# Edge scores of a graph attention layer: row one-hots made three sets ahead, and pieces of rows handed back a step later

## The reference, cut to what matters

```python
Q = relu(x @ query_kernel + query_bias)[row]      # one row of 128 per edge
K = relu(x @ key_kernel + key_bias)[col]
att = sum(Q.reshape(-1, 8, 16) * K.reshape(-1, 8, 16), axis=-1)   # 8 scores per edge
alpha = segment_softmax(att, row, 6250)
```

## Time and profile before

| what | value |
|---|---|
| median of three runs | 10467.82 us |
| the profiled execution's own time | 10462.73 us |
| its span | 10461.2 us |
| the stage, first to last VectorE one-hots or reduce | 2342.9 to 3404.8 us |
| VectorE busy in 2342 to 3405 us | 972.79 us of 1063 |
| TensorE busy in the same stretch | 925.54 us |
| ScalarE busy in the same stretch | 664.03 us |
| GpSimd busy in the same stretch | 55.06 us |
| granted TensorE clock in the stretch | 1.00 |

### The profile page before, as it was taken

One profiled execution on the slowest core, in us unless ns is written; L12 is line 12 of the kernel. 1 busy time (PEld: TensorE's weight loads), 2 busy tenths in 40 slices (PEclk: granted clock), 3 DMA queues, 4 the chain that ended last, 5 costly groups with the idle time before them and its releaser, 6 DMA issues. The chain is left out here.

```text
span 10461.2 us, 308127 instructions
## 1 busy us (share of the span) xinstructions
PE 8085.6 (77%) x93666; PEld 6641.9 (63%) x93814; DVE 8031.5 (77%) x16702; ACT 4527.8 (43%) x9123; POOL 1394.2 (13%) x1711
## 2 busy tenths in 40 slices
PE   2335666758888456999986998898999779579996
PEld 0232225547777446999984666346999746378886
DVE  4987777779999666666667998777888777788887
ACT  0220002236666114666654443786777556323333
POOL 0110001210000002666550000000000012100000
PEclk7555555559999557999998999999999989889998
DMA  2000004424444112333324887785555400000000
GB/s 55 0 7 8 5 5 141 147 77 163 161 162 155 38 37 81 123 123 121 124 95 162 271 273 245 259 292 159 144 144 144 115 5 6 3 4 3 3 3 14
DMA packets 613317, 1065.91 MB, mean 102 GB/s; under 512 B 120883, under 2 KB 266554, under 8 KB 606967
## 3 DMA queue, kind: packets, MB, share of 16 engines
q1 hardware_dynamic: 489222, 890.58, 26.8%
q10 hardware_dynamic: 113040, 161.93, 4.2%
q0 software_dynamic: 10976, 12.53, 0.4%
HBM read 868.94 MB, written 195.84 MB: 102 GB/s over the span
## 5 line engine op out<-in xcount | busy, mean ns | idle before, releaser
L2548 POOL TENSOR_TENSOR acc<-acc,m_sum 128x544 f32<-128x544 f32 (+1 forms) x637 | 811.0, 1273 | 1225.5 <-ACT m_sum L2515 1185.2
L2412 DVE TENSOR_TENSOR m_msg<-m_vps,m_msg 128x512 f32<-128x512 f32 (+1 forms) x637 | 427.7, 671 | 409.4 <-PE m_vps L2453 371.2
L2477 PE MATMUL m_sps<-m_msg,m_oh 128*128 128x136 f32 x4900 | 697.5, 286 | 0.0
L2884 PE MATMUL u_sps<-u_r,u_oh 128*128 128x129 f32 x4900 | 657.2, 275 | 28.7 <-ACT u_r L2840 28.7
L1545 ACT COPY sp_adj_x<-sp_aps_x 128x512 f32<-128x512 f32 (+1 forms) x637 | 363.0, 570 | 724.2 <-PE sp_aps_x L1516 724.2
L1532 PE MATMUL sp_out_x<-x,sp_adj_x 128*128 128x128 f32 x4802 | 672.8, 284 | 0.0
L1516 PE MATMUL sp_aps_x<-sp_ohw_x,sp_oh_x 128*128 128x128 bf16 x7350 | 537.3, 221 | 166.1 <-DVE sp_ohw_x L1483 166.0
L2117 PE MATMUL s_qps<-q_parts,s_oht 128*128 128x128 bf16 x7203 | 511.5, 220 | 198.6 <-DVE s_oht L1599 146.9
L2868 PE MATMUL u_zps<-fcs,u_a 128*128 128x128 f32 x4916 | 655.1, 276 | 7.2 <-ACT u_a L2833 7.2
L2884 PEld LDWEIGHTS u_sps<-u_r,u_oh 128*128 128x128 f32 x4900 | 599.0, 192 | 37.6 <-issue 37.6
L2477 PEld LDWEIGHTS m_sps<-m_msg,m_oh 128*128 128x128 f32 x4900 | 609.9, 190 | 0.0
(11 more groups left out here) (590 smaller groups left out, 19682.3 us busy)
## 6 DMA issues: line engine op xcount, KB each, us to landing
u_e<-e_tiles SPq DMA_DIRECT2D x591, 256.0 KB, 2.8
e_tiles<-t_es ACTq DMA_DIRECT2D x588, 256.0 KB, 4.2
g_e<-e_tiles SPq DMA_DIRECT2D x588, 256.0 KB, 4.5
s_rows<-bucket_rows SPq DMA_DIRECT2D x148, 768.0 KB, 4.1
m_rows<-bucket_rows SPq DMA_DIRECT2D x148, 768.0 KB, 4.1
bs_krow<-bucket_keys SPq DMA_DIRECT2D x49, 1600.0 KB, 7.0
t_rows<-bucket_rows SPq DMA_DIRECT2D x148, 384.0 KB, 5.2
s_rows<-bucket_rows SPq DMA_DIRECT2D x49, 896.0 KB, 5.1
```

Source lines behind the costliest of these rows:

```text
L2477: last = nc.tensor.matmul(sps[x][:, at:at + M], oh[x][:, j * P:(j + 1) * P], msg[x][:, j * M:(j + 1) * M], start=True, stop=True)
L2548: nc.gpsimd.tensor_tensor(at, at, sums[x][:, 0:n * M], ALU.add).then_inc(added, 1)
L2884: last = nc.tensor.matmul(sps[:, :], oh[x][:, j * P:(j + 1) * P], zr[x][:, j * D1:(j + 1) * D1], start=(q == 0 and j == 0), stop=(q == las ...
```

## The change

The one-hots are made for step q + 3 and no longer for q + 2 (`AHEAD = 3`), in the same ring of three slots and a spare one; three sets are made ahead of the first window. Handing a piece back (the waits for `oht_made` and `act_made`, and the increment of `rows_free`) becomes a function of its own, `give_back`, which runs behind the reduce of the same step and no longer between the one-hots and the reduce. For the first three sets it runs ahead of the loop. On ScalarE the wait for the ring slot (`k_made`) moves from ahead of Square to ahead of Relu, and both work for step q + 3.

```diff
-    last_q = NQ - 1
+    last_q, AHEAD = NQ - 1, 3
@@ vector
                     else:
                         row_hots(nc, k, B, oht[r], buf[n], q).then_inc(oht_made[r], 1)
+
+                def give_back(w, q):
+                    n, r = piece_of(B, q), O.slot(q)
                     if q + 1 == B.pieces[n][1]:
                         dve.wait_ge(oht_made[r], O.before(w, q) + 1)
                         here = [p for p in shared if p < B.pieces[n][1]]
                         if here:
                             dve.wait_ge(act_made, w * len(shared) + (len(here) + 1))
                         dve.sem_inc(rows_free[n], 1)
...
-                first_hots(0)
-                first_hots(1)
+                for q in range(AHEAD):
+                    first_hots(q)
+                for q in range(AHEAD):
+                    give_back(0, q)
                 with dve.Fori(0, nw) as w:
...
                         nc.vector.tensor_tensor(prod[x]..., qs[x]..., kps[x]..., ALU.mult).then_inc(prod_made[x], 1)
-                        if q + 2 < NQ:
-                            hots(w, q + 2)
-                        else:
-                            hots(w + 1, q + 2 - NQ)
+                        wp, p = (w, q + AHEAD) if q + AHEAD < NQ else (w + 1, q + AHEAD - NQ)
+                        hots(wp, p)
                         dve.wait_ge(prod_made[x], X.before(w, q) + 2)
                         n = B.held(q)
                         nc.vector.tensor_reduce(...).then_inc(summed[x], 1)
+                        give_back(wp, p)
@@ scalar
-                        p, n = q + 2, w * len(shared)
+                        p, n = q + AHEAD, w * len(shared)
                         if p in shared:
-                            back, user = O.user_before(p)
                             act.wait_ge(rows_in[piece_of(B, p)], w * 16 + 16)
-                            act.wait_ge(k_made[X.slot(user)], X.before(w, user) + (1 + k0 + back * X.uses[X.slot(user)]))
                             act.wait_ge(act_made, n + (shared.index(p) + 1))
                             nc.scalar.activation(far[:, :], row_of(1, p), ACT.Square, bias=minus[:, 0:1]).then_inc(far_made, 1)
                         act.wait_ge(q_made[x], X.before(w, q) + 1)
                         act.wait_ge(prod_made[x], X.before(w, q) + 1)
                         nc.scalar.copy(qs[x]..., qps[x]...).then_inc(q_copied[x], 1)
                         if p in shared:
+                            back, user = O.user_before(p)
                             act.wait_ge(far_made, n + shared.index(p) + 1)
+                            act.wait_ge(k_made[X.slot(user)], X.before(w, user) + (1 + k0 + back * X.uses[X.slot(user)]))
                             nc.scalar.activation(oht[O.slot(p)][:, GE:], far[:, :], ACT.Relu, bias=1.0, scale=-1.0).then_inc(act_made, 1)
```

## The result

The changed kernel takes 10409.68 us (median of 5 runs, 10406.45 to 10416.37) against 10465.63 us of the kernel before in the same comparison (5 runs): a ratio of 0.9946, 95% interval 0.9932 to 0.9961. It is faster by 56 us. The forecast was 87 us faster, 10381 us; the measured time lies just past the end of the range, 10408. The direction and the mechanism named for the gain hold, the size does not: 31 us are missing.

What follows compares the result with a forecast made beforehand. VectorE was taken to bound the stage, but for one wait per window at its seam. Four hand-backs of 0.445 us save 1.78 us per window, 87 us over 49: 10467.8 - 87 = 10381 us, range 10370 to 10408.

Steps and rivals of the forecast that it cites:

- The value of the hand-back: VectorE: handing back behind the reduce saves 0.445 us at four places per window, 87 us over 49 windows.
- the slow one-hots beside GpSimd's copy: VectorE one-hots taking 0.57 for 0.48 us beside GpSimd's copies: forecast to stay; if they missed, 4 us more won.
- One-hots three ahead ... I cost this at nothing: TensorE's waits for one-hots go, but VectorE didn't wait on them, so the longer lead was priced at nothing.
- The seam stays: From multiply 12 to multiply 0 of the next window: k group 0 still waits for multiply 12, 1.51 us as before.
- I take nothing: Waits of a hand-back, now ahead of the next multiply, cost nothing; a satisfied wait at most 0.02 us.
- the forecast period of 19.83 us: Time from multiply 0 to multiply 0 of the next window: 21.61 us less 1.78 us for four hand-backs.
- my third rival: At the seam, TensorE's longer pause lets the clock fall and the kernel gets slower, up to 10980 us; chance 0.02.
- the 1.9 us of pause: At the seam, TensorE finishes q group 0 earlier and waits about 1.9 us for multiply 12, where it paused 1.34.
- the slack of 3.7 us per window: TensorE's spare time per window: its groups need 16.1 us against VectorE's new 19.83.
- The first rival: Part is taken back: hand-back instructions not quite hidden, or step 1 late after the seam; 10409 to 10425 us, chance 0.12.
- ScalarE's Relu ahead of copy 1: First step after the seam: Relu delays copy 1, margins 0.15 to 0.2 us; priced at nothing, 10 us kept for range.
- TensorE's 146.9 us of waits for one-hots: TensorE's waits for VectorE's one-hots, forecast to go with three sets ahead, at no gain to VectorE.

Runs made afterwards that it cites:

- The filler: Changed kernel plus 24 matmuls nobody reads, between q and k group of step 0: 10394.44 us, ratio 0.9938; with 8 matmuls 10399.99 us.
- piece 0 later: Changed kernel, but piece 0 is handed back behind the reduce of step 0 of the next window, not of step 12: 10412.76 us, ratio 0.9952.
- the slot alone: Changed kernel plus a ring slot of its own for step 12, so step 0 doesn't wait for multiply 12: 10383.12 us, ratio 0.9927.
- slot and later hand-back: Changed kernel with a ring slot of its own for step 12 and piece 0 handed back a step later: 10374.35 us, ratio 0.9907.
- the longer pause: Two sets ahead, only the hand-back moved, but the q group of step 0 waits for the reduce of step 12: 10474.55 us, ratio 1.0004.

## Why the prediction was wrong

**The value of the hand-back was right.** 87 us were forecast; alone it brought 92 us, and the reduce's waits of 68.5 us are gone. The remaining 4 or 5 us are the slow one-hots beside GpSimd's copy: with sets two ahead they now miss it (step 11 takes 1.58 us there and 1.68 before), which I had kept as a possible 4 us. In the changed kernel they still meet it (1.66). The Trainium skill, page "VectorE: DVE Perf Modes", section "The DRAIN you can't avoid", says that a semaphore after each of a chain of VectorE instructions costs nothing extra, by which the self-wait would be free. Here the stage got 90 us shorter, 4 of them by the slow one-hots, which leaves 0.44 us for each of 196 places, so the measurement decides against that rule for a wait in front of another instruction of VectorE.

**The step that failed is "One-hots three ahead ... I cost this at nothing", together with "The seam stays" and the "I take nothing" for the moved waits, where it was applied to the one at the loop's end.** Against the forecast period of 19.83 us three terms were missing:

1. Falls of the clock. They were my third rival, at its place, but I had put it at 0.02, counted it only from nine groups per window on, where the kernel is slower than before, and argued from TensorE's share over the whole stage. They came at 13 of 48 seams at 1.2 us: 15 us. The filler took out just these. The price per group (0.64 us; 0.5 to 0.65 measured) and the 1.9 us of pause (1.75 measured) were near; I didn't add the two shorter pauses at the same place, and I took the slack of 3.7 us per window as if it lay at the seam, where there is none.
2. The loop's end. Seam 1.69 for 1.51 us, 0.18 x 49 = 9 us. I had priced the waits of a hand-back behind a reduce at nothing, with 0.02 us as the most, and did so for all four. The one behind the reduce of step 12 isn't like the others: its cover is a reduce of 0.41 us, and the loop's end stands behind it; which of the two matters no run parts. In the changed kernel k group 0 is done at the same place as before, and multiply 0 comes 0.18 us later. The kernel with piece 0 later showed it in its undisturbed windows, and the slot alone (1.70 us, no other engine named) against slot and later hand-back (1.33 us) showed it again.
3. Steps 0 and 2, 1.52 and 1.51 for 1.45 us, 6 us in all. In step 0 the reduce starts 0.23 us behind the multiply's end and not 0.17; in step 2 the next multiply starts 0.66 behind the reduce and not 0.60. Both stay with the filler and with piece 0 later (1.52 and 1.54 us in the latter). They are not one thing: with sets three ahead and a slot of its own for step 12, step 2 takes 1.45 us again, while step 0 stays at 1.52. Step 2 holds a hand-back, so its 0.06 us may be a wait that isn't quite hidden; what holds either step stays open.

15 + 9 + 6 = 30 of the 31 us. The first rival (part is taken back, 10409 to 10425) gave nearly the measured number, mostly by luck: one hand-back isn't quite hidden, as it said, which is 9 of the 31 us, but half is the clock, which it didn't name, and ScalarE's Relu ahead of copy 1, which I had feared, held nobody.

**What the lead of three was worth.** I had said that TensorE's 146.9 us of waits for one-hots would go. That was misread: 69.1 us are one wait ahead of the first window, and it stays. What went are the other 97 waits of 77.8 us, and 97 more for the half sets of L2069:

```profile
PE s_qps L2117 <- DVE s_oht L2069: 45.8, 97, 0.5
```

They brought VectorE nothing, as forecast. Yet they had a use: they spread TensorE's idle time over the window. With them gone, TensorE runs into the seam early and stands there in one place.

## What to carry to other kernels

Removing waits from an engine that isn't the bound can cost time: the same idle time gathers where a dependency can't be moved (1.59 us at the seam before, 2.82 with three ahead alone), and the clock can fall there for work that has no slack behind it. So price such an edit at its new place, adding up all pauses around it. Hand buffers back behind work that covers it, but not as the last thing ahead of a loop's end; and run the parts of a change separately, since here one part was worth 92 us and the other, alone, minus 33.

## What the runs showed of the hardware

A wait of VectorE for its own last instruction, with the next instruction queued behind, costs 0.43 to 0.46 us each time: 0.35 of idle time and 0.09 of lost overlap. Behind a reduce of 0.68 us it costs 0.01 at most in all four places of the kernel with the hand-back alone (steps of 1.60, 1.45, 1.59 and 1.45 us, where steps without one take 1.59 or 1.45).

With no other engine in the way, VectorE needs 1.33 us from the multiply of step 12 to that of step 0, where its work is 1.06 (0.33 + 0.40 + 0.33 by the start-to-start distances). By this estimate about 0.27 us is left for the end of the loop and the waits at its start; no run parts these. The Trainium skill, page "Advanced Engine Details and Errata", section "Control Flow Timing", gives about 108 ns for a compare-and-branch; no run here shows a branch by itself, and by that figure it would be less than half of what is left.

The falls come at the same place with the same pauses in front, yet in only some windows: in the changed kernel the seams with a fall and those without have the same range of idle time, 2.26 to 2.49 us. They come at even distances, in every second window with three ahead alone, in every third or fourth of the changed kernel (third, now and then second, with piece 0 later and with the longer pause). Why it is these windows stays open here.
